# Decoder of two layers on one core: the projection, value and output jobs of the first self-attention get other places among the 64 score tiles of a sequence

## The chip, the cores and the metric

The kernel runs on one core of a Trainium2 chip. The metric is the device time of one execution in microseconds (us). A time that is shown for a kernel is the median of several executions.

## The reference

Four sequences of 512 rows with 256 channels go through six parts, each added to a residual: self-attention, cross-attention to a context of 1601 rows, a mixture of experts, and the same three again with other forms. The change touches the first part alone:

```python
x = x + _L0_attn_ref(_layernorm(x), ...)          # 16 heads of 16 channels
qkv = x @ in_proj_weight.T + in_proj_bias
bias = minimum(rel * slopes, 8.0)                 # rel = query position - key position
scores = einsum('bhqd,bhkd->bhqk', q, k) * D ** -0.5 + bias
probs = softmax(scores)
out = einsum('bhqk,bhkd->bhqd', probs, v)
return out @ out_proj_weight.T + out_proj_bias
```

## The kernel before

`run` calls one stage after the other; an all-engine barrier closes each. `self_attention` is the first after `constants`. Its work is an order written out by hand, which every engine walks in the same way, and semaphores tie the engines together.

**Tiles.** A score tile is 128 keys by 512 queries of one head of one sequence. Four heads make a group of 16 tiles (four key tiles t, four heads each), a sequence has 4 groups or 64 tiles, and there are 256 tiles. This text calls the sequences 0 to 3, and numbers the tiles of one from 0 to 63; `l` in the code is that number, `n` the number over all.

**The loop over tiles.** For tile n, TensorE (PE) computes the scores (L655) into one of three PSUM banks, then does the jobs that `at(n)` names, then the scores of tile n+22 a second time with queries and keys changed over (L625, bank ring MB of three), from which VectorE (DVE) takes the maximum of each query. After every fourth tile come the products with the values for the four tiles before (L637, `values`). DVE adds the band of the position bias where the tile has one (L784), does its share of the jobs, and takes the maxima of tile n+22 (L755 with the bias strip for heads 0 to 10, L758 for the others). ScalarE (ACT) takes the exponential (L714), then its share of the jobs. Score tile n needs the exponential of tile n-3; the maxima matmul of tile m needs the maxima of m-3. Tiles of heads 0 to 7 nearly all have a band, those of 8 to 10 some, those of 11 to 15 none: 38 of 64.

**Jobs.** They all use one PSUM bank, JB, and one after the other: PE starts a job when the one before has been read out (`job_done`).

- p (four for a sequence): the projection of half of the queries or keys of the next sequence, in the order queries 0, keys 0, queries 1, keys 1. PE L594; ACT writes `FULL` (L678) and its rounded part `HI` (L681); DVE writes the rest, `LO` (L733). DVE stands at LO until ACT has written HI.
- v (two): the values of the next sequence, PE L598, read out by DVE (L739).
- o (two): the output projection of the sequence before, PE L613, added to X by DVE (L745).
- a (two): transposes ahead of o. turn (one for a group, at its tile 6): PE L606 transposes `RAISED`, which ACT has copied (L700) after the exponential of tile 4; DVE divides by the sums (L765, L768). row (one for a group, at its tile 11): PE L602, ACT writes `ROW` and sends it by DMA into the queries, for which the first score tile of the next group waits.

**The way of the queries and keys.** The SP queue runs, for each sequence b, `store_half(b, 0)`, `stack_keys(b, 0)`, `stack_queries(b, 0)`, `store_half(b, 1)`, `stack_keys(b, 1)`, and `stack_queries(b, 1)` to `(b, 3)`. `store_half` waits for LO of its two projections and writes HI and LO to DRAM (L514, L515); `stack_keys` waits until they are there and loads six pieces (L524); `stack_queries` issues eight loads (L535, L537) for a group. The maxima matmuls of the next sequence's group 0 begin at tile 42 of the current one (64 - 22) and want keys half 0 and the queries of group 0; those of its group 1 begin at tile 58 and want `stack_queries(b, 1)`, which stands behind everything of half 1. Groups 2 and 3 have their maxima from tiles 10 and 26 of the next sequence on.

GpSimd (POOL) meanwhile splits context and weights for later stages and moves them through DRAM on a queue of its own.

Of the kernel before, what the change touches and what calls it, by code (L numbers as in the profile page):

```python
# [56 lines left out]
class Core:  # L57
# [340 lines left out]
    def self_attention(self):  # L398
# [6 lines left out]
        nc, a, bank, X = self.nc, self.a, self.bank, self.X  # L405
# [27 lines left out]
        def at(n):  # L433

            b, l = n // PB, n % PB
            jobs = []
            if b + 1 < B:
                jobs += {1: [("p", b + 1, 0)], 3: [("p", b + 1, 1)], 17: [("p", b + 1, 2)], 19: [("p", b + 1, 3)],
                         34: [("v", b + 1, 0)], 37: [("v", b + 1, 1)]}.get(l, [])
            if b >= 1:  # L440
                jobs += {13: [("a", b - 1, 0)], 15: [("a", b - 1, 1)], 25: [("o", b - 1, 0)], 29: [("o", b - 1, 1)]}.get(l, [])
            if n % GN == 6 and n >= GN:
                jobs.append(("turn", n // GN - 1, 0))
            if n % GN == 11 and n // GN + 1 < NG:
                jobs.append(("row", n // GN + 1, 0))
            return jobs

        after = [("turn", NG - 1, 0), ("a", B - 1, 0), ("a", B - 1, 1), ("o", B - 1, 0), ("o", B - 1, 1)]
        order = before() + [("row", 0, 0)] + [x for n in range(N) for x in at(n)] + after
        place = {x: i for i, x in enumerate(order)}  # L450

        with self.room() as sb:
# [29 lines left out]
            with self.stage() as (sem, ctx):  # L482
# [102 lines left out]
                def _(pe):  # L585
# [63 lines left out]
                    for n in range(N):  # L649
                        g, t, h = tile_of(n)  # L650
                        if n >= 3:
                            pe.wait_ge(probs, n - 2)
                        if n % GN == 0:
                            pe.wait_ge(row_in, 32 * (g + 1))
                        pe.matmul(SB[n % 3][:, :], keys(h)[:, t * P:(t + 1) * P], queries(h),  # L655
                                  start=True, stop=True).then_inc(sc_ready, 1)
                        for x in at(n):
                            job(x)
                        if n + LEAD < N:
                            maxima(n + LEAD)  # L660
                        if n % GH == GH - 1 and n >= GH:
                            values(n // GH - 1)
# [5 lines left out]
                def _(act):  # L668
# [37 lines left out]
                    for n in range(N):  # L706
                        g = n // GN
                        if n >= RING:
                            act.wait_ge(used, n // GH - 1)
                        if banded(n):  # L710
                            act.wait_ge(biased, bands[n + 1])
                        else:
                            act.wait_ge(sc_ready, n + 1)
                        act.activation(PR[:, n % RING, :], SB[n % 3][:, :], ACT.Exp).then_inc(probs, 1)  # L714
                        for x in at(n):
                            job(x)
                        if n % GN == 4 and g >= 1:
                            raise_outputs(g - 1)
# [1215 lines left out]
```

## Time and profile before

| | us |
|---|---|
| median of 3 runs | 3141.96 |
| lowest and highest | 3135.05, 3144.26 |
| the profiled execution, its own time | 3139.22 |
| span in its trace, first to last instruction | 3137.4 |
| busy over the span: PE, DVE, POOL, ACT | 2805.0, 1855.2, 1662.9, 1302.2 |
| exponential of score tile 0 to that of tile 255 (L714), in the trace | 162.1 to 469.8 |

The trace is of one execution; times in it run from its first instruction. An instruction that overlaps the end of the one before has a mean duration above the step from start to start, so steps are read as differences of starts. PEclk is the granted share of TensorE's clock: 1.00 is 2.4 GHz, 0.50 is 1.2 GHz.

### The profile page before, as it was taken

How to read it: one execution, taken by the hardware profiler on the slowest of the kernel's cores; microseconds unless marked ns; L12 is line 12 of the kernel's file. 1: busy time of each engine (PE TensorE's matmuls, PEld its weight loads, DVE VectorE, ACT ScalarE, POOL GpSimd, SP SyncE). 2: the span in 40 equal slices, each digit the busy share in tenths (PEclk: the TensorE clock that was granted, in tenths of full speed). 3: DMA queues.
4: the chain of work that ended last, by engine and by line, in shares of the span. 5: the costliest groups of instructions: out<-in, count | busy, mean ns of one | idle time of the engine just before them, and what ended most of it. 6: DMA issues, size and time to landing. Idle time of an engine off the chain costs nothing. (4 is left out here: it accounts for less than half of the span.)

```text
span 3137.4 us, 38375 instructions
## 1 busy us (share of the span) xinstructions
PE 2805.0 (89%) x12634; PEld 1764.7 (56%) x12634; DVE 1855.2 (59%) x3754; ACT 1302.2 (42%) x2326; POOL 1662.9 (53%) x1406
## 2 busy tenths in 40 slices
PE   5688886999999999587999999999999999999979
PEld 5344445555565665454656556665656556556557
DVE  2466766665767665446555556556556555556456
ACT  1155564444455455122444444444444444444410
POOL 2144403665666667502466666666666666666710
PEclk8789998999999999797999999999999999999979
DMA  8655613232332321002223232224222233222110
GB/s 278 132 152 163 157 33 109 64 102 51 103 75 54 97 63 32 34 0 73 60 69 74 53 99 68 52 68 106 53 67 68 54 97 75 57 63 63 32 54 27
DMA packets 114229, 245.51 MB, mean 78 GB/s; under 512 B 16239, under 2 KB 62576, under 8 KB 112881
## 3 DMA queue, kind: packets, MB, share of 16 engines
q1 hardware_dynamic: 107824, 219.52, 27.4%
q0 software_dynamic: 5696, 23.42, 2.7%
q8 instruction: 102, 1.67, 0.2%
q14 instruction: 95, 0.77, 0.1%
q10 hardware_dynamic: 512, 0.13, 0.0%
HBM read 106.98 MB, written 31.80 MB: 44 GB/s over the span
## 5 line engine op out<-in xcount | busy, mean ns | idle before, releaser
L1049 POOL TENSOR_TENSOR ACC<-ACC,PR 128x512 f32<-128x512 f32 (+1 forms) x1056 | 1331.0, 1282 | 456.2 <-ACT PR L1274 448.2
L1274 ACT ACTIVATE PR<-banks 128x512 f32<-128x512 f32 (+1 forms) x832 | 468.8, 597 | 669.2 <-PE banks L1163 668.2
L1335 DVE TENSOR_REDUCE mx<-banks 128x2 f32<-128x800 f32 (+1 forms) x512 | 504.1, 986 | 393.6 <-PE banks L1115 392.0
L1179 PE MATMUL banks<-PR,V 128*64 128x512 f32 (+1 forms) x2496 | 599.1, 604 | 0.0
L1162 PE MATMUL banks<-QA,KA 128*128 128x512 f32 (+1 forms) x1248 | 535.5, 429 | 12.3 <-DMA QB<-ROW 11.5
L1115 PE MATMUL banks<-KH,QZ 128*128 128x400 f32 (+1 forms) x1536 | 480.7, 372 | 41.2 <-DVE mx L1335 20.8
L1163 PE MATMUL banks<-QB,KB 65*128 65x512 f32 (+1 forms) x1248 | 495.2, 397 | 0.0
L1115 PEld LDWEIGHTS banks<-KH,QZ 128*128 128x128 f32 x1536 | 267.9, 189 | 225.6 <-issue 89.7
L1274 ACT ACTIVATE PR<-banks,small 128x512 f32<-128x512 f32 (+1 forms) x416 | 269.4, 687 | 300.3 <-PE banks L1163 290.1
L1332 DVE CUSTOM_DVE_ANT_0 banks<-banks,maskadd 128x400 f32<-128x400 f32 (+1 forms) x512 | 289.2, 588 | 143.6 <-PE banks L1115 136.8
L1303 DVE TENSOR_TENSOR KB<-banks,KH 64x400 fp32r<-64x400 f32 (+1 forms) x384 | 219.4, 571 | 260.0 <-ACT KH L1207 254.5
L1162 PEld LDWEIGHTS banks<-QA,KA 128*128 128x128 f32 (+1 forms) x1248 | 231.0, 185 | 224.2 <-issue 192.8
L1049 POOL TENSOR_TENSOR ACC<-PR 128x512 f32<-128x512 f32 x96 | 121.1, 1281 | 343.8 <-ACT PR L1274 343.8
L1179 PEld LDWEIGHTS banks<-PR,V 128*64 128x64 f32 (+1 forms) x2496 | 154.0, 136 | 260.9 <-issue 241.0
L1163 PEld LDWEIGHTS banks<-QB,KB 65*128 65x128 f32 (+1 forms) x1248 | 231.6, 186 | 32.1 <-issue 11.0
L1067 PE MATMUL banks<-CX,WK 128*128 128x400 f32 (+1 forms) x960 | 221.5, 362 | 14.0 <-DVE KB L1303 6.3
L1079 PEld LDWEIGHTS banks<-WV,CX 128*128 128x128 f32 (+1 forms) x1560 | 204.4, 184 | 11.5
L1079 PE MATMUL banks<-WV,CX 128*128 128x256 f32 (+1 forms) x1560 | 210.7, 280 | 0.0
L1067 PEld LDWEIGHTS banks<-CX,WK 128*128 128x128 f32 x960 | 179.6, 195 | 47.0 <-DVE QA L1310 18.0
L714 ACT ACTIVATE PR<-banks 128x512 f32<-128x512 f32 x256 | 144.2, 600 | 135.1 <-DVE banks L784 107.4
L1342 DVE RECIPROCAL RD<-RD 128x128 f32<-128x128 f32 x192 | 172.5, 928 | 35.3 <-ACT RD L1199 34.4
L755 DVE CUSTOM_DVE_ANT_0 banks<-banks,strip 128x512 f32<-128x512 f32 x176 | 119.3, 705 | 25.1 <-PE banks L625 24.4
(243 smaller groups left out, 2977.4 us busy)
## 6 DMA issues: line engine op xcount, KB each, us to landing
KA<-KH SPq DMA_DIRECT2D x192, 400.5 KB
CX<-ctx_split SPq DMA_DIRECT2D x8, 2403.0 KB, 10.4
WK<-wk_split SPq DMA_DIRECT2D x48, 256.0 KB, 5.7
WV<-wv_split SPq DMA_DIRECT2D x24, 512.0 KB, 3.9
QA<-QZ SPq DMA_DIRECT2D x96, 128.0 KB
QB<-QZ SPq DMA_DIRECT2D x96, 128.0 KB
first<-in_w_in SPq DMA_DIRECT2D x8, 1024.0 KB, 6.2
second<-in_w_out1T SPq DMA_DIRECT2D x8, 1024.0 KB, 8.8
```

Of the source, the lines that this page charges most:

```text
L1049: pool.tensor_tensor(acc, other, PR[0:r, n % RING, :], ALU.add).then_inc(summed, 1)
L1067: last = pe.matmul(J[:, 0:w], W[:, u, :], CX[:, v, o:o + w], start=(n == 0), stop=(n == 4))
L1079: last = pe.matmul(J[0:r, o:o + 2 * P], CX[:, v, t * P:t * P + r], WV[:, u, :], start=(n == 0), stop=(n == 4))
L1115: pe.matmul(bank_at[:, 0:w], QZ[:, h, t * P:(t + 1) * P], KH[:, o:o + w], start=True, stop=True).then_inc(mx_ready, 1)
L1162: pe.matmul(SB[n % 3][0:r, :], KA[:, par, h, t * P:t * P + r], QA[:, par, h, :], start=True, stop=False)
L1163: pe.matmul(SB[n % 3][0:r, :], KB[:, par, h, t * P:t * P + r], QB[:, par, h, :], start=False, stop=True).then_inc(sc_ready, 1)
L1179: last = pe.matmul(OB[h * DH:(h + 1) * DH, :], V[0:r, g % 4, s, h * DH:(h + 1) * DH], PR[0:r, (n + h) % RING, :], start=(s == 0), stop=(s ...
L1274: act.activation(PR[0:r, n % RING, :], SB[n % 3][0:r, :], ACT.Exp, bias=keybias[0:r, g // pairs, t:t + 1] if masked else 0.0).then_inc(pro ...
L1303: last = dve.tensor_tensor(KB[0:DH, par, h, o:o + w], J[hd, 0:w], KH[hd, o:o + w], ALU.subtract)
L1332: dve.tensor_tensor_reduce(b, b, maskadd[:, g // pairs % 2, o:o + w], 1.0, -BIG, ALU.add, ALU.max, out).then_inc(mx_done, 1)
L1335: dve.tensor_reduce(mx[:, :, t, c], couples[i % 2 if g == 0 else 0][:, :, 0:w], AX.X, ALU.max).then_inc(mx_done, 1)
L1342: dve.reciprocal(part, part).then_inc(inverted, 1)
```

## The change

In `at(n)` the tile numbers of the jobs are other ones. The projections go from tiles 1, 3, 17, 19 to 2, 18, 33, 45, the values from 34, 37 to 50, 61, and the output projections from 25, 29 to 35, 56. The jobs a, turn and row stay. Nothing is computed in another way, no instruction is added or removed, and the SP queue keeps its order.

```diff
--- before.py
+++ after.py
@@ -435,10 +435,10 @@
             b, l = n // PB, n % PB
             jobs = []
             if b + 1 < B:
-                jobs += {1: [("p", b + 1, 0)], 3: [("p", b + 1, 1)], 17: [("p", b + 1, 2)], 19: [("p", b + 1, 3)],
-                         34: [("v", b + 1, 0)], 37: [("v", b + 1, 1)]}.get(l, [])
+                jobs += {2: [("p", b + 1, 0)], 18: [("p", b + 1, 1)], 33: [("p", b + 1, 2)], 45: [("p", b + 1, 3)],
+                         50: [("v", b + 1, 0)], 61: [("v", b + 1, 1)]}.get(l, [])
             if b >= 1:
-                jobs += {13: [("a", b - 1, 0)], 15: [("a", b - 1, 1)], 25: [("o", b - 1, 0)], 29: [("o", b - 1, 1)]}.get(l, [])
+                jobs += {13: [("a", b - 1, 0)], 15: [("a", b - 1, 1)], 35: [("o", b - 1, 0)], 56: [("o", b - 1, 1)]}.get(l, [])
             if n % GN == 6 and n >= GN:
                 jobs.append(("turn", n // GN - 1, 0))
             if n % GN == 11 and n // GN + 1 < NG:
```

## Rows read from the trace of the kernel before

**Rows 1.** Windows of L714, tiles 0-23, sequences 0-3: length, ACT busy, PEclk, DMA.

```profile
162.08:202.53 40.45, 14.23 (x24) 0.86 0.65 182
242.47:284.03 41.56, 14.23 (x24) 0.88 0.66 180
326.37:366.24 39.87, 14.25 (x24) 0.91 0.64 181
409.81:434.87 25.06, 14.20 (x24) 1.00 0.04 11
```

**Rows 2.** The same for tiles 24-31 (sequences 0, 3) and 32-39 (2, 3).

```profile
202.53:210.39 7.86, 4.49 (x8) 1.00 0.53 128
434.87:445.53 10.66, 4.56 (x8) 1.00 0.01 2
376.90:387.36 10.46, 4.68 (x8) 1.00 0.64 159
445.53:453.11 7.58, 4.62 (x8) 1.00 0.00 0
```

**Rows 3.** Timeline of sequence 2, tiles 1 to 6: PE, ACT, DVE.

```profile
326.03 0.39 PE L655 MATMUL banks<-QS,KS 128*128 128x512 f32 x1
328.20 0.40 PE L655 MATMUL banks<-QS,KS 128*128 128x512 f32 x1
329.55 0.69 DVE L733 TENSOR_TENSOR LO<-FULL,HI 128x512 fp32r<-128x512 f32 x1 [2.38 <-ACT HI L681]
331.20 0.60 ACT L714 ACTIVATE PR<-banks 128x512 f32<-128x512 f32 x1 [1.68 <-DVE banks L784]
336.78 0.63 PE L606 MATMUL banks<-ident,RAISED 128*128 128x128 f32 x4 [3.28 <-ACT RAISED L700]
```

**Rows 4.** Timeline of sequence 3: scores 2, exponential 3, turn; scores 33, exponential 34.

```profile
409.92 0.39 PE L655 MATMUL banks<-QS,KS 128*128 128x512 f32 x1
412.38 0.60 ACT L714 ACTIVATE PR<-banks 128x512 f32<-128x512 f32 x1 [0.24 <-DVE banks L784]
414.45 0.63 PE L606 MATMUL banks<-ident,RAISED 128*128 128x128 f32 x4 [0.89 <-ACT RAISED L700]
...
445.18 0.40 PE L655 MATMUL banks<-QS,KS 128*128 128x512 f32 x1
447.17 1.08 ACT L714 ACTIVATE PR<-banks 128x512 f32<-128x512 f32 x2 [0.20 <-DVE banks L784]
```

**Rows 5.** Windows: busy time by engine and clock after a turn, and late.

```profile
337.50:340.80 3.30, 3.30 (x12) 0.99 (x11) 2.15 (x7) 0.93 (x2) 1.91 (x3) 0.50 0.70 191
366.00:470.00 104.00, 94.38 (x485) 48.66 (x483) 71.64 (x197) 61.45 (x118) 18.14 (x18) 1.00 0.28 61
```

**Rows 6.** Timeline of PE, sequence 1: scores of tiles 45, 46, 48 and 58.

```profile
308.79 0.39 PE L655 MATMUL banks<-QS,KS 128*128 128x512 f32 x1
309.25 0.39 PE L655 MATMUL banks<-QS,KS 128*128 128x512 f32 x1
311.26 0.50 PE L655 MATMUL banks<-QS,KS 128*128 128x512 f32 x1
319.40 0.39 PE L655 MATMUL banks<-QS,KS 128*128 128x512 f32 x1
```

**Rows 7.** Timeline of SP and PE: half 1 to group 1, sequence 0.

```profile
139.72 0.43 SPq L515 DMA_DIRECT2D parts<-LO  x1
153.23 1.22 PE L625 MATMUL banks<-KS,QS 128*128 128x512 f32 x2 [2.18 <-DMA QS<-q_rows]
```

**Rows 8.** Lines L515 and L524: DMA to landing, us, min/median/max.

```profile
DMA to landing us min/median/max: 2.3/3.6/7.5
DMA to landing us min/median/max: 2.6/4.7/7.1
```

**Rows 9.** Timeline: LO of sequence 0's tile 1, and tile 48 of sequence 2.

```profile
167.41 0.81 DVE L733 TENSOR_TENSOR LO<-FULL,HI 128x512 fp32r<-128x512 f32 x1 [4.28 <-ACT HI L681]
394.23 0.47 PE L655 MATMUL banks<-QS,KS 128*128 128x512 f32 x1 [0.70 <-DMA QS<-ROW]
```

## Prediction

> **What bounds the kernel now.** I read the page first: over the whole span PE is the busiest engine, but the change lives in a tenth of it, so I went to the stage. There I cut each sequence's 64 exponentials into four stretches and compared the same stretch of the four sequences with windows, since they differ just in their jobs. Tiles 0 to 23 take 40.45, 41.56 and 39.87 us where four projections stand in them and 25.06 us in sequence 3, which has none [rows 1]. The reader is to see that a projection costs some 3.7 us here, far more than its own work on PE. Tiles 24 to 31 take 7.86 us without output projections (sequence 0) and 10.66 with two: 1.40 each. Tiles 32 to 39 take 7.58 us without value jobs and 10.46 with two: 1.44 each [rows 2].
>
> The timeline says why. In sequence 2 the scores of tile 1 are at 326.03 and the projection behind them; LO starts at 329.55, after DVE stood for 2.38 us while the product, FULL and HI were made in turn, and the next exponential comes at 331.20 [rows 3]. Tiles with a band are paced by DVE, so its standing counts in full. Then the turn: PE has run ahead as far as its rings let it and stands for 3.28 us until RAISED comes [rows 3], and in the stretch right after that its granted clock is 0.50, 1.2 GHz, with PE busy all the time [rows 5]. Without projections it stands for 0.89 us before the same job [rows 4] and the clock stays at 1.00 throughout [rows 5]. From about tile 40 on PE paces: scores follow each other by 0.46, and by 2.01 over two tiles with the products of the values between (309.25 to 311.26 [rows 6]), with no idle time noted before any.
>
> **The change part by part.** Terms are in us, made against the profiled execution (3139.22 by its own time, 1.82 outside its span, 2.74 under the median).
>
> *Tiles 0 to 23.* Two projections stay, at 2 and 18. In sequence 2 LO starts 3.52 after the scores of its tile and the next exponential 1.65 after LO, 5.17 in all [rows 3]. Tile 2 of sequence 3 has its scores at 409.92, so with a projection the exponential of tile 3 would come at 415.09 where it is at 412.38 now [rows 4]: 2.7 each. Before the turn PE now waits two or three times for under 1.2 us, not once for 3.3, so I take no low clock there. The forecast of a stretch is 25.06 + 5.4 = 30.5: sequence 2 gains 9.4; sequence 1 gains 11.1, of which I leave 0.7 for one LO slowed by POOL's work; sequence 0 starts on the low clock, its first LO is waited for 4.28 [rows 9], 1.9 more than 2.38, and it has about 1.1 of a start-up still to pay: 33.5, a gain of 7.0. Together -26.8.
>
> *Tiles 24 to 31.* The output projections leave sequences 1, 2 and 3: 3 x 2.80 = -8.4.
>
> *Tiles 32 to 39.* The value jobs leave (-2.88 each for sequences 0 to 2); the projection at 33 comes. By the same 5.17 the exponential after it comes at 445.18 + 5.17 = 450.35 where it is at 447.17 [rows 4], 3.2 later, of which DVE, with fewer bands to add here, gives a little back: +3.0 in sequence 0. With the output projection at 35 behind it, PE's own work decides: a job moves the next score tile by 2.17 - 0.46 = 1.71 (326.03 to 328.20 [rows 3], against 0.46 without one [rows 6]), two by 3.4 (FULL has emptied the job bank before the second wants it), and DVE's addition a further 0.2: +3.6 in sequences 1 and 2. Sequence 3 has the output projection alone, +1.7. Together -8.6 + 3.0 + 7.2 + 1.7 = +3.3.
>
> *Tiles 40 to 63.* Here PE has nothing to hide a job behind. The value jobs at 50 and 61 and the output projection at 56 cost 1.71 each: sequence 0 has 3.4, sequences 1 and 2 have 5.1, sequence 3, with the output projection alone and no maxima left to take, 1.4. The projection at 45 costs 1.71 and a ring stall: its LO comes 3.52 after scores 45, LO and the maxima of tile 67 take 0.7 each, to 4.9, and PE wants that bank right after scores 48, 311.26 - 308.79 + 1.71 + 0.2 = 4.4 [rows 6], so +0.5. That is 2.2 for each of three. Against it tile 48 of sequence 2 no longer waits 0.70 for ROW [rows 9]: -0.7. Sum 3.4 + 10.2 + 1.4 + 6.6 - 0.7 = +20.9.
>
> *The hand-over.* Keys of half 1 are now made at tile 45 rather than 19, and group 1 wants its queries, behind them in SP's queue, at tile 58. Nothing in the loop of before shows this wait, but the start of the stage does: from the store of LO at 139.72 to the first maxima matmul of group 1 at 153.23, for which PE waited, 13.5 [rows 7]. The store would be issued 4.6 after scores 45 (3.52, LO's own 0.69, and the store of HI ahead of it), so all is there 18.1 after them. PE arrives at 319.40 - 308.79 + 0.2 = 10.8 [rows 6] plus the jobs: 2.2 + 1.7 = 3.9 makes it 14.7 in sequence 0, and with the output projection 16.4 in sequences 1 and 2. So 13.5 gives waits of 3.4, 1.7 and 1.7. Bounds: none, since that chain of the start had eight more loads of SP close behind it, which now come later; and 6.3 more each, with the longest landings of store and keys, 7.5 and 7.1 in place of 3.6 and 4.7 [rows 8]. I take 2.5, 0.9 and 0, half-way down for the first two and nothing where POOL's transfers are nearly over: +3.4. Behind this matmul stand all of PE's later scores, so ACT and DVE run dry within the three banks and the wait counts in full. Further down SP's queue the loads of groups 2 and 3 move back too, but these are wanted only from tiles 10 and 26 of the next sequence on, so I cost them at nothing; the same goes for keys 0 at tile 18, wanted at tile 42.
>
> The Trainium skill, "DMA: Bandwidth & Descriptors", section "Anatomy of one DMA", puts the fixed cost of a DMA at about 2.0 us, most of it until the write is confirmed. By it (an estimate) store and last load would take 4 us beside 6 us of issuing, all would be there 15 us after scores 45, and only sequence 0 would wait, 0.3: the whole would come out 3 us lower. The trace differs: the landings have medians of 3.6 and 4.7 us [rows 8].
>
> *Sum.* -26.8 - 8.4 + 3.3 + 20.9 + 3.4 = -7.6; I round to -7.5. Nothing else waits on the stage's end than the next stage, so it passes on. Forecast 3141.96 - 7.5 = 3134.5.
>
> **The rivals.**
>
> *A: the queries of group 1 are there in time and PE hides more.* For it: the lower bound of the hand-over. Against: in sequence 0 PE arrives 3.4 ahead of the traced chain. Without the wait (3.4) and the ring stall (1.5) it is -12.4: 3129.5.
>
> *B: the low clock stays.* PE's waits before the turns are split but still add up to over 2 us within some 3. A low stretch of 3.3 us with PE busy throughout [rows 5] costs at most half of it, 1.65, and I take 1.3, as DVE's pace hides some. Six turns give 7.8, hence +0.3: 3142.3. Against it: with a wait of 0.89 the clock holds [rows 4, 5]. The skill's page "TensorE: Matmul & The Clock Gate", section "What's actually happening", says that the gate follows how busy PE has been recently, not one gap, which would let split waits count together and speaks for B; the traced stretches have only the two extremes, so none decides between them.
>
> *C, the other side: the hand-over is long.* If store and keys land as late as the longest rows, every sequence waits 6.3 more at tile 58: 19 more, and a low clock behind each wait, 4. That is -7.5 + 23 = +15.5: 3157.5. It makes the kernel slower by over 0.3% from some 20 us of waits in all, 6.8 for a sequence. Against: the medians are far below these maxima [rows 8].
>
> *D: the change only shifts costs.* If the late projections cost 3.7 as the early ones do, not 2.2 and 3.0, it is 3 x 1.5 + 0.7 x 3 = 6.6 more: -0.9, 3141. For it: LO is made by the same chain; against: only tiles with bands make DVE's standing count in full.
>
> **How the numbers follow.** 0.3%, 9.4 us, is about what a measurement of this kernel can tell from no change. Forecast 0.45, its own range 3129 to 3139; A 0.19; B 0.15; D 0.11; C 0.06; 0.04 for what I have not thought of. Faster by over 0.3% (below 3132.5): A nearly whole, 0.17, and the lower part of the forecast, 0.12: 0.29. Slower (above 3151.4): C and half of the rest, 0.08. Same: 0.63. The range is 3127 to 3146: A, B and D lie inside, C outside, with a little of A below.
>
> **What the changed profile would show.** The exponentials 0 to 23 at about 33.5, 30.5, 30.5 and 25.1 us; no clock of 0.50 around the turns at 6 and 22, and PE's idle before L606 near 1 us; tiles 24 to 31 at 7.9 in all sequences; tiles 40 to 63 longer by some 8 us in sequences 0 to 2; a wait of L625 for QS<-q_rows at tile 58, largest in sequence 0. What would make me wrong: that wait far above 2.5 us, low clock after the turns, or LO waits in late tiles that PE does not cover.

## The result and the profile after

The changed kernel takes 3155.68 us (median of 4, 3155.27 to 3156.49), the kernel before 3142.02 in the same comparison. The ratio is 1.0048, 95% interval 1.0034 to 1.0062: slower by 0.5%, some 13.7 us at the medians, where 7.5 less was forecast. The profiled execution took 3156.05, span 3154.3. The time lies outside the range of the prediction, on the side of its rival C.

The same four stretches of each sequence's exponentials, read as for the kernel before. Windows of L714 in the changed kernel: from and to, length, ACT busy, granted clock, DMA share, GB/s. First tiles 0 to 23 of sequences 0 to 3, which answer to [rows 1]; then 24 to 31 and 32 to 39, which answer to [rows 2]; then 40 to 63.

```profile
159.13:190.68 31.55, 14.23 (x24) 0.91 0.45 137
251.49:285.02 33.53, 14.24 (x24) 0.95 0.54 157
339.43:370.45 31.02, 14.17 (x24) 1.00 0.58 147
420.42:445.48 25.06, 14.21 (x24) 1.00 0.04 11
...
190.68:202.05 11.37, 4.50 (x8) 1.00 0.84 179
285.02:296.37 11.35, 4.50 (x8) 0.91 0.86 172
370.45:379.24 8.79, 4.46 (x8) 1.00 0.80 179
445.48:453.31 7.83, 4.49 (x8) 1.00 0.01 3
...
202.05:214.12 12.07, 4.58 (x8) 0.86 0.43 145
296.37:309.75 13.38, 4.62 (x8) 0.82 0.42 116
379.24:390.35 11.11, 4.58 (x8) 1.00 0.62 196
...
214.12:251.49 37.37, 13.35 (x24) 0.86 0.63 161
309.75:339.43 29.68, 13.34 (x24) 1.00 0.56 158
390.35:420.42 30.07, 13.16 (x24) 1.00 0.58 112
```

Tiles 40 to 63 were not shown for the kernel before; its windows of L714 for sequences 0, 1 and 2 are

```profile
220.84:242.47 21.63, 12.62 (x24) 1.00 0.48 136
305.16:326.37 21.21, 12.61 (x24) 1.00 0.43 119
387.36:409.81 22.45, 12.62 (x24) 1.00 0.55 132
```

Summed over the sequences, and with sequence 3's last stretches (9.31 against 7.58, and 17.8 against 16.7 up to the last exponential), against the forecast:

| tiles | forecast | measured | difference |
|---|---|---|---|
| 0 to 23 | -26.8 | -25.8 | +1.0 |
| 24 to 31 | -8.4 | -0.5 | +7.9 |
| 32 to 39 | +3.3 | +6.9 | +3.6 |
| 40 to 63 with the hand-over | +24.3 | +33.0 | +8.7 |
| sum | -7.6 | +13.6 | +21.2 |

The reader is to see two things. The first stretch gained what was forecast. And of sequences 0 to 2, the one in which PE never waits long, sequence 2, is within about 1.0 of its forecast in each stretch, while 0 and 1 lose much in tiles 24 to 39, and 0 in 40 to 63.

What ended there comes out of PE's rows. At tile 32 of the changed kernel the first scores of the new group wait for ROW, in sequence 0 and 1:

```profile
201.16 0.47 PE L655 MATMUL banks<-QS,KS 128*128 128x512 f32 x1 [3.50 <-DMA QS<-ROW]
...
295.19 0.77 PE L655 MATMUL banks<-QS,KS 128*128 128x512 f32 x1 [3.15 <-DMA QS<-ROW]
```

and 0.89 in sequence 2. The timeline of ACT and SP shows what the load of ROW met. ROW is copied at 193.62 and sent at 193.90; SP is issuing the six loads of keys and eight of queries behind the projection at tile 18 just then, and ROW is in the queries only at 201.16, 7.3 us after its copy ended. For the three row jobs that run during sequence 3, with hardly any other transfers, the scores follow 3.5 to 4.9 after the copy and wait for nothing, so without other transfers ROW needs no more than that.

```profile
193.62 0.25 ACT L686 ACTIVATE ROW<-banks 16x128 fp32r<-16x128 f32 x1
193.90 1.28 ACTq L690 DMA_DIRECT2D QS<-ROW  x2
...
189.98 2.66 SPq L524 DMA_DIRECT2D KS<-parts  x6
192.76 1.28 SPq L535 DMA_DIRECT2D QS<-parts  x3
194.09 0.28 SPq L537 DMA_DIRECT2D QS<-q_rows  x1
194.41 2.66 SPq L535 DMA_DIRECT2D QS<-parts  x3
197.11 0.28 SPq L537 DMA_DIRECT2D QS<-q_rows  x1
```

At tile 58 of sequence 0 comes the hand-over, rows of SP and PE:

```profile
222.89 0.43 SPq L515 DMA_DIRECT2D parts<-LO  x1
229.28 2.66 SPq L524 DMA_DIRECT2D KS<-parts  x6
235.54 1.24 SPq L535 DMA_DIRECT2D QS<-parts  x3
...
240.98 0.80 PE L625 MATMUL banks<-KS,QS 128*128 128x512 f32 x1 [7.54 <-DMA QS<-q_rows]
```

From the store of LO to the maxima of group 1 it took 18.1 us, where [rows 7] had 13.5: the store was in DRAM after 6.4 (229.28 - 222.89), and the loads took 11.7. PE stood for 7.54. The third row begins the eight loads of group 2, which SP issues while the queries of group 1 are still on their way. In this execution sequence 1 waited 0.10 there and sequence 2 not at all.

With these waits the clock falls. Windows of the changed kernel with busy time of PE, PEld, DVE, ACT and POOL, then the clock: around tile 58 of sequence 0, and from tile 32 on in sequences 0 and 1.

```profile
236.30:246.40 10.10, 5.42 (x16) 2.08 (x17) 1.52 (x4) 0.98 (x3) 4.47 (x6) 0.50 0.68 206
202.20:205.40 3.20, 3.20 (x5) 1.24 (x4) 0.59 (x2) 1.05 (x2) 2.82 (x4) 0.50 0.00 0
294.40:301.00 6.60, 5.81 (x10) 3.30 (x11) 1.20 (x3) 1.91 (x4) 4.41 (x6) 0.50 0.16 35
```

Both waits put the projection at 33 on the half clock: in sequence 0 it fills PE for 3.44 us where it took 1.88 at the full one.

```profile
201.93 3.44 PE L594 MATMUL banks<-HTA,w 128*128 128x512 f32 x4
```

Of the span's difference, 16.9, the stage's loop has 13.6. The first tile came 3.0 earlier, and what follows the last exponential took 6.2 longer, 3.9 of it up to the end of the output projections that close the stage: they ran on the half clock, 3.78 and 3.71 where they took 1.99. Whether those 3.9 belong to the change is open. From the last exponential to the end of these projections it is 15.4 to 15.5 us in the changed kernel and in the traces of e1_p_only and e9_last_at_45 below, 12.9 to 13.1 in six of the other eight, and 11.4 in e3_o_only, e8_p_early and the kernel before. The timed difference, 13.7, agrees with the loop's; each trace is one execution, so that is no proof of its own.

### The profile page after: what moved, and what is told of

Its sections match the earlier page's. It is cut to its first block and busy times, and to the rows that moved or that the text cites. A ratio compares the mean times of both kernels' runs of the same rounds, so it can differ in the third digit from the quotient of the medians.

```text
span 3154.3 us, 38375 instructions
## 1 busy us (share of the span) xinstructions
PE 2815.8 (89%) x12634; PEld 1766.9 (56%) x12634; DVE 1855.8 (59%) x3754; ACT 1304.0 (41%) x2326; POOL 1662.1 (53%) x1406
## 5 line engine op out<-in xcount | busy, mean ns | idle before, releaser
L1079 PEld LDWEIGHTS banks<-WV,CX 128*128 128x128 f32 (+1 forms) x1560 | 204.6, 184 | 11.4
L1067 PEld LDWEIGHTS banks<-CX,WK 128*128 128x128 f32 x960 | 179.1, 195 | 47.3 <-DVE QA L1310 18.2
L714 ACT ACTIVATE PR<-banks 128x512 f32<-128x512 f32 x256 | 145.8, 598 | 143.0 <-DVE banks L784 91.1
L625 PE MATMUL banks<-KS,QS 128*128 128x512 f32 x256 | 121.5, 486 | 20.7 <-DMA QS<-q_rows 14.1
```

What stands on the lines that cost most here:

```text
L1067: last = pe.matmul(J[:, 0:w], W[:, u, :], CX[:, v, o:o + w], start=(n == 0), stop=(n == 4))
L1079: last = pe.matmul(J[0:r, o:o + 2 * P], CX[:, v, t * P:t * P + r], WV[:, u, :], start=(n == 0), stop=(n == 4))
```

## The experiments

Each kernel differs only in tile numbers. A diff below shows them for projections (p), values (v) and output projections (o), with `-` for the kernel it departs from. e1 to e4 were timed beside the kernel before at a median of 3137.98, e5 to e8 at 3141.29, e9 and e10 at 3140.04; the changed kernel itself was timed only with its result, so it is compared with them by the ratios. Single runs of the kernel before spread over 3128 to 3155, so a verdict on the time rests on the ratio's interval. The waits are read from one execution of each kernel, and that one can lie far from the kernel's median: 7.5 above it for e1, 7.4 for e5 and 10.6 for e9, 6.0 below it for e3, 7.7 for e4 and 9.1 for e6. Which waits occur is therefore safer to say than how long they are.

**One part of the change at a time, and the change with one part undone.**

```diff
 e1_p_only (kernel before, projections moved)
-p 1 3 17 19
+p 2 18 33 45
 e2_v_only (kernel before, values moved)
-v 34 37
+v 50 61
 e3_o_only (kernel before, output projections moved)
-o 25 29
+o 35 56
 e4_o_back (changed kernel, output projections back)
-o 35 56
+o 25 29
```

> The projections alone at 2, 18, 33, 45; values and output projections where they were. Theory W (the gain of tiles 0 to 23 is eaten by waits for loads that the moved projections cause: the queries of group 1 at tile 58, ROW at tile 32): tiles 0 to 23 gain 26; tile 32 has no wait in sequences 1 and 2, where the output projection at 29 still covers it, and 3 us in sequence 0; 33 and 45 cost 3 x 3.0 and 3 x 2.2; with no job at 50 and 56 PE comes to tile 58 earlier, so it waits about 9 there in sequence 0 and 3 in the others. In all +5 against the kernel before, 3147. Theory P (the loss is made by the value and output jobs at tiles where PE has no slack): the projections alone gain 11, 3131.

Measured: 1.0038 (1.0024 to 1.0053), median 3149.94. Theory P falls: the projections alone make the kernel slower, by 12 at the medians where theory W gave 5. Rows of PE at tile 32 of sequence 0 and at tile 58 of sequences 0, 1 and 2:

```profile
202.04 0.47 PE L655 MATMUL banks<-QS,KS 128*128 128x512 f32 x1 [3.85 <-DMA QS<-ROW]
...
240.38 0.79 PE L625 MATMUL banks<-KS,QS 128*128 128x512 f32 x1 [5.58 <-DMA QS<-q_rows]
...
329.98 0.80 PE L625 MATMUL banks<-KS,QS 128*128 128x512 f32 x1 [5.80 <-DMA QS<-q_rows]
...
418.93 0.80 PE L625 MATMUL banks<-KS,QS 128*128 128x512 f32 x1 [3.87 <-DMA QS<-q_rows]
```

Without the jobs at 50 and 56 PE is at tile 58 earlier and all three sequences wait, 15.3 in all where 15 was expected. Theory W had tile 32 free of waits in sequences 1 and 2, and they waited 0.91 and 2.0 in spite of the output projection at 29: that part of it was too kind.

> The value jobs alone at 50 and 61. Theory W: they cost 1.71 each where they cost 1.44 before, six of them, +1.6: 3143.6. Theory P: they cost some 3 each there, +9: 3151.

Measured: 1.0004 (0.9994 to 1.0015), median 3140.46. The loop took 308.8 us by its trace against 307.7. Theory P's 9 lies above the interval; theory W's 1.6 lies inside it, and so does nothing at all.

> The output projections alone at 35 and 56. Theory W: tiles 24 to 31 gain 8.4, 35 and 56 cost 9.9 in all, and ROW is waited for at tile 32 in sequences 1 to 3, but shortly, 1 each, since no loads of SP run then: +4.5, 3146.5. Theory P: no wait for ROW, the jobs cost 3 each at their new places: +9, 3151.

Measured: 1.0031 (1.0020 to 1.0043), median 3149.59, 9.7 above the kernel before by the ratio: more than theory W's 4.5 and level with theory P's 9. But theory P had no wait, and ROW is waited for at tile 32, 3.85 in sequence 1 (12.22 us for tiles 24 to 31 and 14.47 for 32 to 39, clock 0.88) and 0.55 in sequence 2. I had written that no loads of SP run then; they do: in the kernel before too the keys behind the projection at 19 are loaded about tile 24 (issued from 281.97 in sequence 1, whose exponential 24 is at 284.03), and the DMA share in this window is 0.87. That the output projection at 29 merely covered this wait is not the whole of it. In sequence 1 of the kernel before, the scores of tile 32 follow ROW's copy by 4.82 and do not wait, so ROW was there by then; in e3 they follow by 8.12. Without the job at 25 ROW is sent 3.8 after SP begins to issue the keys and no longer 7.0, and its load took over 3 us longer. What the job at 29 covers is smaller: with the wait taken off, the scores of tile 32 follow the copy by 4.9 where it stands there (e1, e4) and by 3.8 where it does not (changed kernel), so 1.1. That is the second half of the fault in my sum: I took 7.86 us, measured in sequence 0, as what is left when these jobs go.

```profile
278.05:290.27 12.22, 4.46 (x8) 1.00 0.87 200
```

> The changed kernel with the output projections back at 25 and 29. Theory W: the one at 29 stands in the wait for ROW at tile 32 and hides it in sequence 1 (3.2 us and the low clock after it, 2.9), sequence 0 keeps its wait; against that the output projections cost 2.8 again in tiles 24 to 31. In all 4 below the changed kernel, 3151.5, still above the kernel before. Theory P: 1.71 to 1.40 each and nothing else, 1.8 below the changed kernel, 3154.

Measured: 1.0050 (1.0031 to 1.0070), median 3156.07, not below the changed kernel's 1.0048. The trace shows what stands against the gain: tiles 32 to 39 did fall to 10.5 in sequences 1 and 2, and ROW's wait in sequence 1 from 3.15 to 1.38 (that of sequence 2 was 1.27), but at tile 58 PE came earlier and waited 2.97, 5.85 and 3.44. One wait was traded for the other.

**Each suspected collision taken away.** Theory W names two: the projection at 45 is too late for tile 58, and the loads behind the projection at 18 delay ROW.

```diff
 e5_p45_at_40 (changed kernel)
-p 2 18 33 45
+p 2 18 33 40
 e6_p18_at_10 (changed kernel)
-p 2 18 33 45
+p 2 10 33 45
 e7_both (changed kernel)
-p 2 18 33 45
+p 2 10 33 40
```

> The changed kernel with its last projection at 40 in place of 45. Theory W: the queries of group 1 are made some 5 us earlier, so the wait of 7.5 us at tile 58 of sequence 0 falls to about 2, the low clock behind it goes or halves, and the runs in which the others wait too get shorter; the waits for ROW at tile 32 (3.5, 3.2, 0.9) stay. Tiles 40 to 63 of sequence 0 take 31 in place of 37. In all 7 below the changed kernel, 7 above the one before: 3145 against 3138. Theory P (the late places cost by PE's lack of slack alone): no change, 40 is as tight as 45: 3152.

Measured: 1.0020 (1.0005 to 1.0035), median 3147.58, 6.3 above the kernel before where theory W gave 7. No sequence waits at tile 58; tiles 40 to 63 of sequence 0 take 30.1. The waits at tile 32 stay, 3.12, 2.05 and 1.72. Theory P falls again.

> The changed kernel with its second projection at 10 in place of 18, so that SP's fourteen loads behind it run at tiles 15 to 22 and not at 24 to 31. Theory W, second half (ROW, sent at tile 27, is late because it shares the DMA engines with these loads): the waits at tile 32 fall from 3.5, 3.2 and 0.9 to under 0.5 and the low clock in tiles 32 to 39 goes, 9 below the changed kernel, 3143 with the kernel before at 3138. Rival R: ROW is late because nothing stands between row and tile 32 any more, whoever else loads: the waits stay at 1 to 3.5 us and the time within 3 of the changed kernel. The wait at tile 58 stays by both.

Measured: 1.0022 (1.0009 to 1.0035), median 3148.43; by the ratios some 8 below the changed kernel where theory W gave 9. Windows of L714 for tiles 24 to 31 of sequences 0, 1 and 2, and the one wait that is left at tile 32:

```profile
194.52:203.00 8.48, 4.50 (x8) 1.00 0.38 100
277.51:285.35 7.84, 4.49 (x8) 1.00 0.34 113
359.32:367.18 7.86, 4.47 (x8) 1.00 0.20 57
...
202.11 0.47 PE L655 MATMUL banks<-QS,KS 128*128 128x512 f32 x1 [0.60 <-DMA QS<-ROW]
```

The stretch falls from 11.37, 11.35 and 8.79 to what I had forecast, with nothing put between row and tile 32; the DMA share in it falls from 0.84, 0.86 and 0.80. Rival R falls: ROW is late where other loads share the engines with it. It does not hang on this one execution: the four traces with a projection at 18 and none at 10 (the changed kernel, e1, e4, e5) have waits of 0.89 to 3.85 at tile 32 in all three sequences, and the two with it at 10 (e6, e7) have 0.60 once each and none else. The scores of tile 32 follow 3.7 to 4.4 us after ROW's copy. At tile 58 the three sequences wait 4.14, 0.46 and 1.56.

> Both of these edits in one. Theory W: both kinds of waits gone, what is left is the sum that I had forecast without its 3.4 of hand-over: 8 below the kernel before, 3130. Rival R: the waits at tile 32 stay, 3138.

Measured: 1.0005 (0.9987 to 1.0024), median 3142.03: both waits are gone (0.73 is left at tile 58 of sequence 0, 0.60 at tile 32 of sequence 2), and with them the loss against the kernel before, but not the 8 more that were expected. What I had missed is in the trace at tile 40: the projection there stands three tiles ahead of row at 43, which wants the maxima that DVE is late with, so tile 40 takes 3.0 instead of 0.5, and tile 43 takes 3.72, 4.36 and 3.53 in sequences 0, 1 and 2, instead of 2.2 to 2.3 in the kernel before; in sequence 1 the clock then falls as well, and at the end of sequence 2 another 1.01 goes on a wait for ROW. Windows of L714, tiles 40 to 63 of sequences 1 and 2, against 29.68 and 30.07 in the changed kernel:

```profile
291.83:324.50 32.67, 13.24 (x24) 0.95 0.61 148
376.30:408.54 32.24, 13.02 (x24) 1.00 0.74 179
```

**The hand-over by itself.**

```diff
 e9_last_at_45 (kernel before)
-p 1 3 17 19
+p 1 3 17 45
```

> The kernel before with its last projection alone moved, from 19 to 45; this takes the hand-over by itself, as SP's loads behind tile 3 stay away from ROW at tile 27. Theory W: tile 19's projection and the low clock behind the pair go, 4.5 in each of three sequences; at 45 it costs 2.4; the queries of group 1 come 18 to 20 us after scores 45 where PE is at tile 58 after 13, so each sequence waits 5 or more there and two of three get a low clock: 13.5 less, 7.2 and 18 more, +12: 3150 with the kernel before at 3138. No wait for ROW at tile 32. Rival L (late queries were an accident of sequence 0): waits under 2, -4: 3134.

Measured: 1.0040 (1.0025 to 1.0054), median 3152.1, 12.1 above the kernel before, as theory W had it. Waits at tile 58 of sequences 0, 1, 2, and none at tile 32:

```profile
239.36 0.79 PE L625 MATMUL banks<-KS,QS 128*128 128x512 f32 x1 [7.40 <-DMA QS<-q_rows]
...
331.16 0.65 PE L625 MATMUL banks<-KS,QS 128*128 128x512 f32 x1 [4.80 <-DMA QS<-q_rows]
...
418.68 0.50 PE L625 MATMUL banks<-KS,QS 128*128 128x512 f32 x1 [2.97 <-DMA QS<-q_rows]
```

The late queries are no accident of sequence 0, nor of one execution: this trace, e1's, e4's and e6's have them in all three sequences.

**Versions built on it.**

```diff
 e8_p_early (kernel before)
-p 1 3 17 19
+p 2 10 18 29
-o 25 29
+o 25 31
 e10_p_2_8_18_29 (e8_p_early)
-p 2 10 18 29
+p 2 8 18 29
```

> A version built on theory W: projections at 2, 10, 18 and 29, values as before at 34 and 37, output projections at 25 and 31. Never two projections before one turn, the loads behind the second run at tiles 15 to 22, those behind the fourth from tile 33 on, and the fourth stands itself in the wait for ROW at tile 32. Tiles 0 to 23 at 33.5 for sequences 0 to 2, tiles 24 to 31 at 12.5, the rest as before: 5 less for each of three sequences, 15 below the kernel before: 3123. Rival R: waits for ROW at tile 32 of 2 more each: 3129.

Measured: 0.9956 (0.9943 to 0.9968), median 3127.9 of 6: 0.44% faster than the kernel before, 13.4 at the medians where 15 was expected, and 0.9% below the changed one. Windows of L714, tiles 0 to 23 of sequences 0, 1, 2, then 24 to 31 of 1 and 2:

```profile
163.87:202.86 38.99, 14.13 (x24) 0.83 0.64 161
245.21:278.37 33.16, 14.16 (x24) 1.00 0.67 190
323.72:358.05 34.33, 14.15 (x24) 0.95 0.65 164
...
278.37:290.93 12.56, 4.56 (x8) 1.00 0.48 169
358.05:370.81 12.76, 4.56 (x8) 1.00 0.48 144
```

Three projections in tiles 0 to 23 cost 8.1 over sequence 3's 25.06 in sequence 1, 2.7 each, as reckoned; the fourth stands in ROW's flight, and nothing waits at tile 32 or 58. Only sequence 0 is dearer than expected.

> The early version with its second projection at 8 in place of 10, three tiles ahead of the row job instead of one. In the early version's trace tiles 0 to 23 of sequence 0 took 39.0 where 33.5 was forecast: behind the projection at 10, row held ACT and PE stood 2.2, and the clock was low for 10 us. Expected: that sequence at 35, the others unchanged, 3 less than the early version: 3124. Rival: its loads now meet ROW of tile 11 and tile 16 waits about 1 in each sequence: 3 more, 3130.

Measured: 0.9982 (0.9969 to 0.9994), median 3135.08: still faster than the kernel before, but worse than projections at 10. Tiles 0 to 23 take 36.8, 36.2 and 36.6. It is neither of the two expectations: sequence 0 gains 2.2, but in the others the projection at 8, right behind the turn and the products of the values, makes tile 8 take 4.87 us where the one at 2 makes its tile take 3.78 (sequence 1), and row at 11 then comes late: PE waits 2.44 for the maxima before it, 0.44 in e8_p_early. Tile 16 waits 0.57 in sequence 0, as in e8_p_early (0.68), and not in the others.

## Why the prediction was wrong

**What bounds it, and tiles 0 to 23: right.** The stretches took 31.55, 33.53 and 31.02. The forecast was 33.5, 30.5 and 30.5, with 0.7 more for sequence 1 in the sum, so -25.8 stands for -26.8. That the sum is so near is partly luck: sequence 0 was 2.0 better than forecast (its first LO was waited for 2.98 and not 4.28), and sequence 1 was 2.3 worse. The turn rows answer to [rows 3]: PE waits 0.92 instead of 3.28 before L606 in sequence 1.

```profile
258.84 0.63 PE L606 MATMUL banks<-ident,RAISED 128*128 128x128 f32 x4 [0.92 <-ACT RAISED L700]
```

Rival B, that split waits still lower the clock, counted six turns; there are five, as sequence 0 has none at tile 6. It took place at one of them, the second of sequence 1 (stretch at 0.95): behind a LO of 2.33 us PE waited 1.89, 0.38 and 0.92, and the clock was 0.50 from 280.61 on. In sequence 0 (0.91) the low stretch, from 167.97 on, stands behind waits of 1.96 and 0.32 after the projection at tile 2, and no turn is near. Neither is the cause of the loss. The Trainium skill's page "TensorE: Matmul & The Clock Gate", section "What's actually happening", which was weighed for this rival, is in keeping with that: split waits can do it, though at four of the five turns they did not.

```profile
274.91 2.33 DVE L733 TENSOR_TENSOR LO<-FULL,HI 128x512 fp32r<-128x512 f32 x1 [2.05 <-ACT HI L681]
```

**Tiles 24 to 31, "the output projections leave, -8.4": the step that failed first.** I took the 7.86 us of sequence 0 as the bare cost of eight tiles. It held for a stretch in which ROW has the DMA engines nearly to itself. I had named row as a job that sends by DMA, but not asked what the moved projections load during its flight, nor how near the loads of the keys ROW comes when the job at 25 goes, nor what the one at 29 covered. Measured -0.5, and with the half clock that follows in tiles 32 to 39, 3.6 more there: 11.5 of the 21.2 us. Experiments e6 (loads away: the wait goes) and e3 (output projections away: the wait comes) show both halves.

**The hand-over, "I take 2.5, 0.9 and 0": the mechanism was right and its size was wrong.** The measure was one 13.5 us chain from the start of the stage; here it took 18.1 in sequence 0. The wait was 7.54 in place of 2.5, and the half clock behind it, for which I had put nothing in the forecast, took the rest of the 7.6 that this sequence lost over its forecast. 7.54 is inside the bounds that the text gave (3.4 + 6.3), so the error was to go down from the traced 13.5 and to let rival C begin only with the longest landings in all sequences. The reason for going down was wrong as well: the eight loads that stood close behind that chain at the start do not come later but stand behind it here too, issued from 235.54 on. C's time, 3157.5, lies near the measured one by luck: of its some 22 us of waits at tile 58 a third took place, and more than half of what the forecast missed is ROW's, which C does not have. What was worked out from the Trainium skill's page "DMA: Bandwidth & Descriptors", section "Anatomy of one DMA", an even shorter chain, was further off: by it sequence 0 would have waited 0.3. That section speaks of DMAs issued by GpSimd, and these are SP's.

**Tiles 32 to 39 and 40 to 63 without the waits: right.** Sequence 2 took 11.11 where 7.58 + 3.6 = 11.2 was forecast, sequence 3 9.31 for 9.3; sequence 1's 40 to 63 took 29.68 for 29.4. The values alone (e2) cost nothing that shows. Rival D, that late projections cost as much as early ones, falls with these numbers, and rival A with the wait at tile 58.

**What stays open.** e4 was expected at 4 below the changed kernel and came out level, which its waits explain, though I have not separated the two waits there. No experiment took SP's loads and POOL's transfers apart, but ROW's flights in the traces do in part. With POOL's queue alone beside it (62.4% of the DMA engines' time in that flight, e6, sequence 0) the scores followed the copy by 4.4; with SP's alone (85.5%, changed kernel, sequence 2) by 4.7; with both (SP 55.8% and 47.3%, POOL 33.1% and 41.9%, changed kernel, sequences 0 and 1) by 7.3 and 6.9. So it is the two together that make ROW late. How long the chain of the hand-over takes from one execution to the next, and whether the low clock behind the stage's last tile hangs on the places of the jobs, stays open.

## What to carry to other kernels

Where jobs are placed by hand, a job has two prices: its own time where it stands, and the flight of the transfers that it starts. Write down for every moved producer when its loads run and which small, urgent load shares the DMA engines with them, and for every removed job which flight it covered. A stretch that is fast without a job in one sequence is no measure for another in which other transfers run; and of a wait that only one traced chain prices, take that chain as the middle and not as the upper end, with the half clock after it as part of the price.

## What the runs showed of the hardware

- ROW's two loads of 4 KB on ACT's queue, from the end of the copy to the scores of tile 32, needed 4.4 us at most with the DMA share of the stretch at 0.20 to 0.38 (e6_p18_at_10), and in the changed kernel 4.7 at 0.80 and 6.9 and 7.3 at 0.86 and 0.84. The last two had both SP's and POOL's transfers beside them, the others one at most.
- LO, one 128x512 instruction of DVE between operands in SBUF, took 0.69 us in the median and 2.33 at the longest, from 274.91; a subtraction of POOL (L574) ran from 274.81 to 276.70. I had left room for 1.38.
- With waits of PE of 3.15, 3.28, 3.50 and 7.54 us the granted clock fell to 0.50 each time; with shorter, split waits before a turn it stayed at 1.00 at four of five, and it fell behind 1.89, 0.38 and 0.92.
